# Attention pipeline: the second norm's two operations at the end of GpSimd's step instead of at its start

## The reference, cut to what matters

```python
ln1 = _ln(hidden_states, ln1_weight, ln1_bias)
qkv = (ln1 @ qkv_weight.T).reshape(S, B, N_KV, (Q_PER_KV + 2) * HEAD_DIM)
...
scores = jnp.einsum('sbhd,tbhd->bhst', q, k) / jnp.sqrt(jnp.float32(HEAD_DIM))
causal = jnp.tril(jnp.ones((S, S), bool))
attn = jax.nn.softmax(jnp.where(causal[None, None], scores, NEG), axis=-1)
attn_out = jnp.einsum('bhst,tbhd->sbhd', attn, v).reshape(S, B, H)
hidden_after_attn = hidden_states + attn_out @ proj_weight.T
x = _ln(hidden_after_attn, ln2_weight, ln2_bias).reshape(-1, H)
probs = jax.nn.softmax(x.astype(jnp.float32) @ router_weight, axis=-1)
```

## Time and profile before

| | us |
|---|---|
| median of 3 runs (8085.17 to 8089.02) | 8086.36 |
| the profiled execution's own time | 8085.06 |
| its span in the trace | 8083.4 |
| PE, DVE, ACT, POOL busy over the span | 6698.1, 4276.0, 3293.0, 4619.2 |
| steps 0 to 86 of the attention stage, about | 4204 to 5026 |

### The profile page before, as it was taken

One profiled execution on the slowest core, in us unless ns is written; L12 is line 12 of the kernel. 1 busy time (PEld: TensorE's weight loads), 2 busy tenths in 40 slices (PEclk: granted clock), 3 DMA queues, 4 the chain that ended last, 5 costly groups with the idle time before them and its releaser, 6 DMA issues. The chain is left out here.

```text
span 8083.4 us, 89638 instructions
## 1 busy us (share of the span) xinstructions
PE 6698.1 (83%) x24560; PEld 3773.2 (47%) x24560; DVE 4276.0 (53%) x5154; ACT 3293.0 (41%) x5916; POOL 4619.2 (57%) x3617
## 2 busy tenths in 40 slices
PE   7888888888889888888969887019999999999920
PEld 3334343333334333333437776006666666666610
DVE  6888888888888888888865566100000000000023
ACT  5555555555555555555536665002222222222200
POOL 6888888888888888888876664660000000000056
PEclk9999999999999999999989998559999999999965
DMA  2333333333333333333333333331111111111146
GB/s 91 126 109 113 118 111 117 109 120 110 121 115 112 117 111 122 107 122 112 114 97 88 105 110 111 128 114 37 49 47 47 36 47 47 36 49 47 36 151 187
DMA packets 518667, 777.03 MB, mean 96 GB/s; under 512 B 62805, under 2 KB 296091, under 8 KB 518352
## 3 DMA queue, kind: packets, MB, share of 16 engines
q1 hardware_dynamic: 449232, 644.78, 24.9%
q0 software_dynamic: 52480, 112.27, 4.4%
q10 hardware_dynamic: 16640, 16.78, 0.6%
HBM read 574.22 MB, written 187.83 MB: 94 GB/s over the span
## 5 line engine op out<-in xcount | busy, mean ns | idle before, releaser
L379 POOL TENSOR_TENSOR m_dbu<-m_du,m_bb 128x1024 f32<-128x1024 f32 x1024 | 2391.2, 2357 | 285.1 <-DMA m_bb<-rows_bc 169.5
L774 PE MATMUL m_y_bank<-m_prod,m_ident 128*128 128x512 f32 x4096 | 2035.1, 623 | 259.2 <-POOL m_prod L389 259.1
L528 ACT ACTIVATE m_decay<-m_delta,m_a_neg 128x512 f32<-128x512 f32 x2048 | 1404.0, 692 | 1184.7 <-DVE m_h L646 1155.4
L774 PEld LDWEIGHTS m_y_bank<-m_prod,m_ident 128*128 128x128 f32 x4096 | 789.1, 198 | 1280.2 <-issue 867.6
L646 DVE TENSOR_TENSOR_SCAN m_h<-m_decay,m_h_end,m_dbu 128x512 f32<-128x512 f32 x1024 | 1268.2, 1269 | 197.9 <-ACT m_decay L528 142.5
L646 DVE TENSOR_TENSOR_SCAN m_h<-m_decay,m_dbu 128x512 f32<-128x512 f32 x1024 | 1209.3, 1210 | 251.6 <-ACT m_decay L528 188.2
L1668 POOL DMA_DIRECT2D slot_out<-e_ye x80 | 60.3, 754 | 2241.8 <-DVE e_ye L1703 2184.4
L1703 DVE COPY e_ye<-e_ybank 128x1024 f32<-128x1024 f32 x80 | 98.0, 1224 | 2248.8 <-PE e_ybank L1737 2248.8
L1737 PE MATMUL e_ybank<-e_w,e_a 128*128 128x256 f32 x5120 | 1126.1, 381 | 0.0
L1729 PE MATMUL e_ubank<-e_xT,e_w 128*128 128x512 f32 x2560 | 1114.7, 593 | 4.1 <-DMA e_w<-in_w 4.1
L1691 ACT ACTIVATE e_a<-e_ubank 128x512 f32<-128x512 f32 x640 | 382.6, 598 | 1764.0 <-PE e_ubank L1729 1764.0
(11 more groups left out here) (183 smaller groups left out, 6655.6 us busy)
## 6 DMA issues: line engine op xcount, KB each, us to landing
m_bb<-rows_bc SPq DMA_DIRECT2D x1024, 256.0 KB, 3.6
m_cb<-rows_bc SPq DMA_DIRECT2D x416, 256.0 KB, 3.3
slot_rows<-m_zeros SPq DMA_DIRECT2D x64, 648.0 KB, 4.5
e_xe<-slot_rows SPq DMA_DIRECT2D x81, 512.0 KB, 3.8
slot_out<-e_ye POOLq DMA_DIRECT2D x80, 512.0 KB, 3.3
m_xin<-in_x SPq DMA_DIRECT2D x32, 512.0 KB, 5.1
m_xres<-in_x SPq DMA_DIRECT2D x32, 512.0 KB, 6.9
x<-m_xres SPq DMA_DIRECT2D x32, 512.0 KB, 4.3
```

Source lines behind the costliest of these rows:

```text
L379: nc.gpsimd.tensor_tensor(dbu[:, slot], du[:, q[1], p * PC:(p + 1) * PC], bb[:, slot].unsqueeze(1).to_broadcast([P, PC, T]), ALU.mult).the ...
L528: nc.scalar.activation(decay[:, cc], delta[:, r, c], ACT.Exp, scale=a_neg[:, c, n:n + 1]).then_inc(decay_done, 1)
L774: ins = nc.tensor.matmul(y_bank[:, cc], ident[:], prod[:, slot, cc], start=False, stop=(n == NS - 1))
```

## The change

In GpSimd's step the call of `inverse_deviation_2` stands behind the other two kinds instead of ahead of them. No operation is added or removed, and no other engine's code changes.

```diff
             for step in range(STEPS):
-                for k in items(step, STATS2):
-                    inverse_deviation_2(k)
                 for k in items(step, STATS):
                     inverse_deviation(k)
                 for k in items(step, VDIAG):
                     place_values(k)
+                for k in items(step, STATS2):
+                    inverse_deviation_2(k)
```

## The result

| | before | changed |
|---|---|---|
| median, us (6 runs each) | 8085.76 | 8138.75 |
| lowest to highest | 8079.06 to 8091.23 | 8129.17 to 8147.25 |
| span of the profiled execution | 8083.4 | 8132.1 |

The ratio is 1.0066, with a 95% interval of 1.0053 to 1.0079: slower by 53 us. The forecast was 8147, 61 us more, the range 8118 to 8166.

A forecast was written before the change was run, and what follows sets the result against it. Bound: a VectorE-GpSimd ring through the value DMAs' landing, 12.7 us a round. Rounds of 14.08 us plus long issues add 64.2 us, ends 0.3, steps 64 to 73 minus 4: 60.5 more, 8147 us, range 8118 to 8166.

The forecast's parts named there:

- The bound before: Steps 23 to 63: VectorE and GpSimd wait for each other through the value DMAs' landing, 12.35 us, 12.7 on average.
- TensorE's 11.4 us: TensorE's busy time per step in steps 23 to 63 of the kernel before, taken as its own pace.
- 14.08: Forecast us for one round of steps 23 to 63 in the changed kernel, against 12.7 before.
- The new ring: Steps 23 to 63: statistics, first norm, eight DMA issues, second norm's power, then VectorE from L1260 to L1197; 14.08 us.
- Statistics: Duration of VectorE's first-norm statistics (L1197 to L1201) in each round: 1.39 us taken, bounds 1.03 and 1.92.
- quiet statistics: Rival: L1094 and DMA issues no longer run beside statistics, round 0.36 us shorter, 46 us more, 8132; chance 0.22.
- The long issues: Three place_values issues in steps 23 to 63 wait 3.2 us each and stay in the round: 8.7 us.
- The ends: Step 23's first norm 3.3 us earlier; L1049 of step 63 to next turn_values 12.60 us, 3.6 more; together 0.3.
- Steps 64 to 73: No first norm there; old round cut, but TensorE nearly full: 4 us off 82.0, bounds 0 and 10.
- The old ring: Kernel before: turn_values to L1252, then GpSimd's L1064, first norm, eight DMAs and their landing; 12.35 us a round.
- The faster case: Rival: normalise_2 (L1260) does not hold up what follows, landing round shrinks to 11.4 us, 39 us less, 8047; chance 0.05.
- TensorE as the pace: Rival: TensorE, busy 90% of steps 23 to 63, hides VectorE's delay, nothing changes, 8086; chance 0.05.

The follow-up runs named there:

- three other orders on GpSimd: Changed kernel with GpSimd's step reordered: first norm, rs2, transfers, 8012.44 us; rs2, transfers, first norm, 8009.47 us; transfers, first norm, rs2, 8010.03 us.

## Why the prediction was right

*The bound before.* Right: the ring through `statistics_2`, rs2, first norm, issues and landing. A second pair of `bn_stats` outside it cost nothing, and taking the first norm out of it (the order rs2, transfers, first norm) made the 40 rounds 75 us shorter. TensorE's 11.4 us as its own pace was wrong by 0.6 us: freed, it does a round in 10.8. That did not touch the forecast, because 14.08 lies above both.

*The new ring.* Right, term by term. In the round shown: the gap 0.09 became 0.08, the first norm to the first issue 3.88 is 3.87, issues 3.91 became 3.93 with the step to L1064, L1064 to L1260 1.02 is 1.03, L1260 to L1197 3.79 became 3.77. Over the 40 rounds the means are 0.08, 4.12, 3.93, 1.03, 3.77 and, for `statistics`, 1.20 us, 14.13 in all. The 4.12 holds the three long issues with 0.22. The two terms tested in size, statistics and the issues, changed the round by about what they changed themselves (0.73 of 0.81 us, and 1.90 of 1.92). The waits came out near the forecast too: L1049 5.1 us each (5.3 forecast), L1260 6.4 (6), TensorE for L1242 2.4 (2.5), and the three rounds with the long issue 17.0, 17.4 and 16.6 us (17).

*Statistics.* This is the term that was mis-sized: 1.39 was taken, and 1.20 measured, by the groups of the changed kernel in 4355:4920:

```profile
L1197 DVE BATCH_NORM_STATS2 a_stats<-a_xa 128x6 f32<-128x256 f32 x80 | 34.6, 473 | 0.0
...
L1201 DVE BATCH_NORM_AGGREGATE a_moments<-a_stats 128x2 f32<-128x6 f32 x81 | 12.0, 189 | 1.4
```

The argument for it was that TensorE, with more slack, would wait for L1242 each time, so that the scores would fall on `statistics` each time. It waited 29 times of 41, and the scores fell on `statistics` less often than before, not more. In the kernel before they begin 0.5 us after its start in 33 of the 40 rounds, and `statistics` takes 1.17 to 1.92 us; in the changed kernel in 21, and it takes 1.20 to 1.77. In all other rounds they begin 0.6 us behind its start or later, and it takes 1.02 or 1.03 us.

What moved them is the clock. The round ahead of the one shown has a wait of TensorE for L1242, and right behind it the lower level (TensorE's rows, then the stretches with the granted clock):

```profile
4693.42 1.09 PE L1322 MATMUL a_side<-a_ident,a_n 128*128 128x128 f32 x4 [2.87 <-DVE a_out_base L1242]
...
4694.98 2.00 PE L1311 MATMUL a_score<-a_kx,a_qT 128*32 128x128 f32 x32
```

```profile
4682.50:4692.80 10.30, 8.05 (x70) 6.92 (x69) 4.08 (x11) 5.80 (x13) 6.67 (x18) 1.00 0.41 123
4692.80:4703.00 10.20, 9.58 (x63) 7.93 (x64) 4.75 (x13) 5.64 (x13) 7.14 (x21) 0.50 0.31 94
4703.00:4713.00 10.00, 10.00 (x114) 8.55 (x113) 7.49 (x18) 6.36 (x12) 4.22 (x13) 1.00 0.33 97
```

`statistics` began at 4693.79 there, and the scores 1.19 us later, because `turn_norm` took 1.09 us instead of 0.6, so it was not stretched. There are 12 rounds like this one, each with a wait of 2.85 us or more and with the scores at 2.0 us instead of 1.3. In the next, the one shown, the clock is back, but TensorE is late from the slow stretch and does not wait. At 4708.10 `turn_back` had only begun, the last `turn_norm` came at 4708.53, after `statistics`, and the scores (L1311, 4709.39) fell on L1248, which is not in the ring and took 1.08 us instead of 0.7. The other seven rounds with a short `statistics` are like that. One round on, TensorE did wait, at the full clock:

```profile
4720.83 0.63 PE L1322 MATMUL a_side<-a_ident,a_n 128*128 128x128 f32 x4 [1.30 <-DVE a_out_base L1242]
4721.39 0.40 PE L1304 MATMUL a_score<-a_causal,a_rows_of 16*32 16x512 bf16 x4
4721.71 1.28 PE L1311 MATMUL a_score<-a_kx,a_qT 128*32 128x128 f32 x32
```

and L1197 at 4721.20 took 1.15 us. The term is 0.19 x 40 = 7.6 us too much in the forecast, and the other terms were 0.8 us too small, so steps 23 to 63 grew by 57.4 us and not 64.2. The rival of quiet statistics was partly right, for a reason that it had not named: it had L1094 and the issues, and what changed is when the scores run.

*The long issues.* Right: three of 3.2 us, in the ring.

*The ends.* Counted from L1049 of step 22, that of step 23 was 3.1 us earlier (3.3 forecast). From L1049 of step 63 to the next `turn_values` it was 12.61 us (12.60).

*Steps 64 to 73.* 4 us off was forecast, and it was 0.8: 81.2 us for the nine rounds against 82.0. The old ring is cut, but TensorE is busy for 77.8 of 82 us at a clock of 0.90, as before. GpSimd's issues now wait for its `outputs` (L1349), 27.2 us in seven steps, and rs2 stands behind those waits in the queue. I had not counted what is queued behind that wait. But that it was 0.8 and not 4 is in part chance. The changed kernel with statistics twice does the same work in these steps, since the first norm is over, and its issues wait there as well (18.9 us in seven steps), but its nine rounds took 75.4 us, at a granted clock of 0.99:

```profile
4986.00:5061.50 75.50, 69.94 (x930) 59.42 (x928) 62.32 (x127) 49.65 (x98) 43.37 (x91) 0.99 0.44 126
```

The forecast had that condition, "unless its clock rises". The rest of the stage, from there to the last L1064, was 0.9 us shorter, which was not forecast. So the whole stage grew by 56 us where 60.5 were forecast. The two main misses, 6.8 us too much in steps 23 to 63 and 3.2 too little in steps 64 to 73, partly made up for each other, which is luck.

*The rivals.* The faster case asked that L1260 not be held up by rs2; it waited 6.4 us on average in each of 40 steps. Statistics first on VectorE is that case made real: what depends on the first norm no longer stands behind L1260, and the cut ring pays, with 90 us. TensorE as the pace was refuted by the second pair of `bn_stats`.

## What to carry to other kernels

In a software pipeline of in-order engines, a wait that is moved back on one engine is moved back for all that stands behind its reader on the other engine. Before moving it, write down the ring that the move closes, with the starts of one round, and compare its length with the ring that it opens. The eight issues, 3.9 us, cost time in the two orders in which they follow the first norm's operations directly and the ring runs through both; in the three others they cost nothing that the time shows. An order that frees one ring can close another: here rs2 last on GpSimd was worth +53 us, statistics first on VectorE nothing, and both together -90. Each of the three other orders on GpSimd did nearly as much alone (-81 to -84).

## What the runs showed of the hardware

- TensorE's granted clock fell behind its longer single waits. In steps 23 to 63 of the changed kernel it waited 17 times for 2.85 us or more for L1242, and in 15 of these cases the clock went to the lower level, 1.2 GHz, within the wait or in the 2 us behind it: 0.88 on average, with 67.4 us of waits for L1242 in all. With statistics twice it was 0.85 (84.6 us). With half of the transfers one such wait was 4.5 us long, the others 1.7 at most: 0.98 (36.1 us). The sum of the waits alone does not tell it: with statistics first on VectorE and GpSimd's order of before they are 35.5 us, twice the 15.7 of the kernel before, the longest 1.6 us, and the clock is 0.99 against 0.98. Nor do these waits tell all: in the kernel before, where none is over 1.0 us, the clock fell six times all the same, and what set that off is open. Busy for all of 431 us (statistics first, GpSimd's order changed): 1.00, that is 2.4 GHz throughout. Where a ring without TensorE set the pace the lower clock cost nothing; it moved TensorE's work against VectorE's, and so the length of `statistics`.
- The issue of a DMA by GpSimd takes 0.49 us, and at long intervals one has 3.2 us of waiting ahead of it for nothing that the profile shows. With eight issues a step this came in steps 27, 42, 57 and 72, in every kernel here that has them: first 128 issues after the stage's first (step 11), then 15 steps, or 120 issues, apart, at rounds from 10.8 to 14.9 us. With four a step it came in step 43, again after 128 issues, and then in step 74, 124 issues on. That fits a count of some 120 issues and not a time. Where TensorE is the bound it is listed with 2.7 to 5.3 us.
- A `bn_stats` pair takes 0.74 us, and up to 1.63 while the scores' matmuls (L1311) run beside it; ScalarE's pair of 128x256 activations 1.09, and up to 2.02. Without the mask matmuls this is nearly the same (1.65 and 1.83). Where neither falls beside the scores, none is longer than 0.75 and 1.09.
